# Graph layers 2 and 3 of a three-part network: second product in three rounded passes, and a new order of each graph's work

## The chip, the cores and the metric

The kernel runs on one core of one Trainium2 chip (trn2). TensorE is called PE below, VectorE DVE, ScalarE ACT, GpSimd POOL and SyncE SP. The metric is the device time of one execution in microseconds, as the median of the runs shown; lower is better.

## The reference

The program has four stages: masked attention, an LSTM, three graph layers, and a product with fp8 rounding. The change touches the graph stage and the load of one weight for the last. For 32 graphs of 256 nodes with 256 features each (D = 256), the graph stage computes

```python
for l in range(3):
    scores = (x @ attn_w[l, :d])[:, :, None] + (x @ attn_w[l, d:])[:, None, :] + attn_b[l]
    scores = jnp.where(scores >= 0, scores, 0.2 * scores)
    attn = jax.nn.softmax(jnp.where(mask, scores, -jnp.inf), axis=-1)
    agg = jnp.einsum('bij,bjd->bid', attn, x)
    h = layernorm(x + agg, g1[l], beta1[l])
    ff = gelu(h @ W1[l] + b1[l]) @ W2[l] + b2[l]      # W1: 256 x 1024, W2: 1024 x 256, all float32
    x = layernorm(h + ff, g2[l], beta2[l])
```

The stage's input is a layernorm of the residual stream, and its output is added to that stream. The last stage, which needs `L1_ffn_weight`, follows.

## The kernel before

`gnn_phase` holds the graph stage: 3 layers of 32 graphs, every tensor of a graph in SBUF. Each engine has its own program, and the order of the work is written out by hand in a function `body` per engine. One body is one graph's turn: `now` is the graph in the wide layer (`up`, gelu, `down`), `ahead` the next one, `soon` the one after, `behind` and `past` the two before. The engines are held together by semaphores alone, and each takes its own instructions in order.

What a graph n goes through: DVE's `as_neighbour` splits the per-node sums into two rounded parts; PE's `scores` (L1384, L1388) adds them to the mask in bank S; ACT's `attend` makes the slope part (Relu, L1086), DVE's `largest` (L1194, L1199) the row maximum, ACT the exponents (L1092); PE's `turn_probs` (L1400) transposes them into bank T, DVE's `turned` (L1211) copies them out; PE's `aggregate` (L1412) multiplies with the nodes; DVE's `aggregated` (L1221, L1227, L1231) adds the residual and takes mean and variance; POOL's `rsqrt1` (four tiny instructions, L975 to L980) makes the scale; ACT's `norm1` (L1116) applies it; PE's `turn_h` (L1421) transposes into bank T again; ACT's `hT_out` (L1138) and DVE's `split_hT` (L1238) turn that into two rounded halves, `hT_upper` and `hT_rest`. Only then may PE write bank T again or start `up`.

`up` (L1447) is W1 times h. Both operands are split into a rounded part of type float32r and the rest, also float32r, and three products are added up (upper x upper, upper x rest, rest x upper), 48 matmuls of 256 columns for a graph. ACT's `feed` (L1104) applies gelu bank by bank, four banks (q = 0 to 3) with two instructions of 256 columns each. `down` (L1464) is W2 times gelu in plain float32: 8 chunks times 2 halves are 16 matmuls, which PE executes as two each, 32 records for a graph. DVE's `feed` (L1265) adds h, `moments2` takes the statistics, POOL's `rsqrt2`, ACT's `norm2` (L1123), and POOL's `scale` and `move` (L1018, L1025) finish the layer.

ACT holds one function table at a time: exponents and gelu need different ones, so each turn has two table loads (at L1082 and L1104). In layer 1 the residual stream of a later graph also enters (POOL `enter`, L1031; `norm_extra`, L1129), and in layer 3 that of a finished graph leaves (POOL `leave`, L1036; L1129). At the edge of two layers `split_w1` (L1246, L1250) rounds the next W1, and PE's `shift_bias` (L1431) multiplies it with one column. `down` has this core, and the PE body this order:

```python
for it in range(NT):
    last = pe.matmul(ff_bank[:, it * D:(it + 1) * D], act1[:, m, it * P:(it + 1) * P], w2[:, m, :], ...)

scores(*ahead); up(*now, range(0, 6)); turn_probs(*ahead); up(*now, range(6, MC))
aggregate(*ahead); down(*now, range(0, 6)); turn_h(*ahead); down(*now, range(6, MC))
```

## Time and profile before

| | us |
|---|---|
| median of 3 runs (lowest to highest) | 3022.4 (3019.73 to 3022.41) |
| profiled execution, its time | 3024.76 |
| its span in the trace | 3023.0 |
| PE matmul busy | 2772.3 (92%) |
| ACT busy | 1784.0 (59%) |
| DVE busy | 1674.8 (55%) |
| POOL busy | 1503.2 (50%) |
| matmuls of `down`, 3072 records | 698.0 |
| matmuls of `up`, 3 x 1536 records | 442.6 + 435.0 + 434.7 |

The graph stage lies from about 1285 to 2906 us of the span. Matmuls are pipelined, so two of them overlap in these sums: the pace of PE is read from the start of one to the start of the next. The shares are averages over the four stages; the time of the graph stage is set by how long one body takes, times 96. TensorE's granted clock is at or near its full level in the graph stage.

### The profile page before, as it was taken

What the parts mean: (1) busy time and instruction counts of PE and PEld (TensorE: products, weight loads), DVE (VectorE), ACT (ScalarE), POOL (GpSimd) and SP (SyncE); (2) the same over time, 40 slices, a digit from 0 to 9 for tenths busy, and PEclk for the clock granted to TensorE, in tenths of its full rate; (3) what the DMA queues carried; (4) which work ended last, traced back from release to release, by engine and by line L of the source; (5) the groups of instructions that cost most, each with busy time, mean ns of one, the idle gap of its engine ahead of it and who ended that gap; (6) DMA issues with size and microseconds to landing.
All of it is one profiled execution on the core that took longest, in us unless ns stands there. A gap on an engine that the chain in (4) does not pass through costs nothing. (4 is left out here: it accounts for less than half of the span.)

```text
span 3023.0 us, 113835 instructions
## 1 busy us (share of the span) xinstructions
PE 2772.3 (92%) x43200; PEld 2452.8 (81%) x43200; DVE 1674.8 (55%) x5581; ACT 1784.0 (59%) x4834; POOL 1503.2 (50%) x2681
## 2 busy tenths in 40 slices
PE   6999999978888888769999999999999999999957
PEld 5777777667777777759889898999999899999956
DVE  6887888634444444446666664544444445454558
ACT  4666666644444444437667665666666577767723
POOL 5777777510000000046666665555555566666644
PEclk9999999999999999979999999999999999999979
DMA  2111111000000000020000011000000100000002
GB/s 88 43 35 35 35 43 35 13 11 12 13 13 12 13 13 13 13 73 26 26 21 26 24 30 48 9 9 7 9 9 7 34 9 9 9 7 9 9 21 90
DMA packets 110487, 72.32 MB, mean 24 GB/s; under 512 B 51424, under 2 KB 109280, under 8 KB 110432
## 3 DMA queue, kind: packets, MB, share of 16 engines
q1 hardware_dynamic: 96464, 58.93, 6.7%
q10 hardware_dynamic: 13968, 12.72, 1.4%
q8 instruction: 27, 0.44, 0.1%
q14 instruction: 28, 0.23, 0.0%
HBM read 50.63 MB, written 20.97 MB: 24 GB/s over the span
## 5 line engine op out<-in xcount | busy, mean ns | idle before, releaser
L1464 PE MATMUL g_F<-g_w,g_act 128*128 128x256 f32 x3072 | 698.0, 380 | 0.0
L1464 PEld LDWEIGHTS g_F<-g_w,g_act 128*128 128x128 f32 x3072 | 578.4, 191 | 75.1
L1447 PE MATMUL g_H<-g_hT_upper,g_w_upper 128*128 128x256 f32 x1536 | 442.6, 288 | 0.0
L1447 PE MATMUL g_H<-g_hT_upper,g_w_rest 128*128 128x256 f32 x1536 | 435.0, 283 | 0.0
L1447 PE MATMUL g_H<-g_hT_rest,g_w_upper 128*128 128x256 f32 x1536 | 434.7, 283 | 0.0
L744 POOL COPY l_xt<-seq 128x64 f32 x256 | 60.9, 238 | 597.5 <-PE l_O L755 595.8
L328 ACT ACTIVATE a_probs<-a_S,a_nmax 128x256 f32<-128x256 f32 x512 | 236.7, 480 | 123.2 <-DVE a_nmax L421 89.8
L1104 ACT ACTIVATE g_act<-g_H,g_small 128x256 f32<-128x256 f32 x768 | 291.4, 490 | 6.0 <-PE g_H L1447 4.8
L1447 PEld LDWEIGHTS g_H<-g_hT_upper,g_w_upper 128*128 128x128 f32 x1536 | 294.5, 192 | 0.1
L1447 PEld LDWEIGHTS g_H<-g_hT_upper,g_w_rest 128*128 128x128 f32 x1536 | 294.5, 192 | 0.0
L1447 PEld LDWEIGHTS g_H<-g_hT_rest,g_w_upper 128*128 128x128 f32 x1536 | 294.5, 192 | 0.0
L783 ACT ACTIVATE l_ic<-l_G 128x128 f32<-128x128 f32 x256 | 71.2, 278 | 342.2 <-PE l_G L755 342.2
L1116 ACT ACTIVATE g_r<-g_r,g_small 128x256 f32<-128x256 f32 x192 | 104.8, 593 | 274.3 <-POOL g_small L980 274.3
L755 PE MATMUL l_G<-wh,l_hT 128*32 128x128 f32 x4096 | 165.3, 279 | 106.5 <-DVE l_hT L817 106.0
L1001 POOL TENSOR_TENSOR g_h<-g_r,g_g_row 128x256 f32<-128x256 f32 x192 | 138.3, 742 | 233.3 <-DVE g_r L1265 233.3
L1238 DVE TENSOR_TENSOR g_hT_rest<-g_T,g_hT_upper 128x512 fp32r<-128x512 f32 x96 | 66.4, 692 | 338.8 <-ACT g_hT_upper L1138 338.8
L755 PEld LDWEIGHTS l_G<-wh,l_hT 128*32 128x32 f32 x4096 | 96.6, 109 | 147.6 <-DVE l_hT L817 147.5
L802 DVE SCALAR_TENSOR_TENSOR l_fresh<-l_ic 128x64 f32<-128x64 f32 x256 | 57.8, 226 | 278.3 <-ACT l_ic L783 278.3
L1018 POOL TENSOR_TENSOR g_r<-g_r,g_g_row 128x256 f32<-128x256 f32 x192 | 135.8, 729 | 146.2 <-ACT g_r L1123 146.2
L978 POOL TENSOR_TENSOR g_small<-g_small,eps_power 128x2 f32<-128x2 f32 x256 | 188.2, 735 | 20.0
L1412 PE MATMUL g_A<-seq,g_probsT 128*128 (+1 forms) x768 | 182.7, 381 | 0.8 <-DVE g_probsT L1211 0.8
L421 DVE TENSOR_REDUCE a_nmax<-a_S 128x2 f32<-128x512 f32 x256 | 157.3, 677 | 15.9 <-PE a_S L590 15.9
(207 smaller groups left out, 7244.3 us busy)
## 6 DMA issues: line engine op xcount, KB each, us to landing
gmask<-masks ACTq DMA_DIRECT2D x97, 128.0 KB, 2.0
x<-in_x_dram SPq DMA_DIRECT2D x32, 256.0 KB, 3.1
a_adj<-in_adj_dram SPq DMA_DIRECT2D x32, 256.0 KB, 2.7
hidden<-l_hs SPq DMA_DIRECT2D x512, 16.0 KB, 1.4
g_hs<-hidden SPq DMA_DIRECT2D x32, 256.0 KB, 2.7
out_dram<-q_res SPq DMA_DIRECT2D x32, 256.0 KB, 2.1
g_w<-in_L_gnn_W_dram SPq DMA_DIRECT2D x6, 1024.0 KB, 6.2
masks<-gmask SPq DMA_DIRECT2D x32, 128.0 KB, 1.7
```

Source lines behind the costliest of these rows:

```text
L328: last = act.activation(probs[h % PROBS][:, it, :], score_bank[h % HG][:, it * N:(it + 1) * N], ACT.Exp, bias=nmax[:, h, it:it + 1], accum ...
L421: dve.tensor_reduce(nmax[:, h, :], score_bank[h % HG][:, :].rearrange("p (t k) -> p t k", t=NT), AX.X, ALU.max, negate=True).then_inc(max_ ...
L755: last = pe.matmul(bank[j * B:(j + 1) * B, 0:(gates.stop - gates.start) * HQ], x[:, c, :], w[:, c, gates, j * HQ:(j + 1) * HQ], start=Fals ...
L783: act.activation(ic[:, :, :], ic_bank[u % 2][:, 0:2 * HQ], ACT.Tanh).then_inc(ic_done, 1)
L978: pool.tensor_tensor(rstd[:, :, 0], veps[:, :, 0], t.power[:, :], ALU.pow).then_inc(rstd_done, 1)
L1001: last = pool.tensor_tensor(h[:, it, :], r1[:, it, :], g1_row[:, :], ALU.mult)
L1018: last = pool.tensor_tensor(r2[:, it, :], r2[:, it, :], g2_row[:, :], ALU.mult)
L1104: last = act.activation(act1[:, 2 * q + i, :], hidden_bank[q][:, i * N:(i + 1) * N], ACT.Gelu, bias=b1_shifted[:, 2 * q + i:2 * q + i + 1])
L1116: last = act.activation(r1[:, it, :], r1[:, it, :], ACT.Identity, bias=nb1[:, it, :], scale=rstd1[:, it, :])
L1412: last = pe.matmul(agg_bank[:, it * D:(it + 1) * D], probsT[:, jt, it * P:(it + 1) * P], t.nodes[:, b, jt, :], start=(jt == 0), stop=(jt = ...
L1447: last = pe.matmul(hidden_bank[m // 2][:, m % 2 * N:(m % 2 + 1) * N], w[:, c, m * P:(m + 1) * P], x[:, c, :], start=(c == 0 and k == 0), s ...
L1464: last = pe.matmul(ff_bank[:, it * D:(it + 1) * D], act1[:, m, it * P:(it + 1) * P], w2[:, m, :], start=(m == 0 and it == 0), stop=(m == M ...
```

## The change

Four things change in `gnn_phase`, and one outside.

1. `down` in layers 2 and 3 takes the form of `up`: `w2_upper`, `w2_rest`, `act_upper` and `act_rest` are float32r, and each of the 16 matmuls becomes three, 48 for a graph. Layer 1 keeps plain float32. The rounded part of the gelus of a bank is made on ACT for the banks in `ON_ACT` (q = 1 and 3 in layer 2, q = 3 in layer 3) and on DVE for the others (`split_act`); the rest is always made on DVE. `split_w2` rounds W2 once a layer, and W2 is loaded in two halves.
2. The turns are reordered. `scores` and the slopes are made for `soon`, and the exponents of `soon` come last but one in ACT's turn, between `norm1(ahead)` and `hT_out(ahead)`; the gelus come first. PE begins a turn with `turn_probs(ahead)`, and `aggregate` stands in the middle of `up`. POOL puts `enter`/`leave` before `rsqrt2`, and `rsqrt1` before `scale`.
3. `scale` writes to `nodes`, so that `r2` is free after `scaled_done`, not after `nodes_done`.
4. W1 of layers 2 and 3 is loaded over the residual stream of four graphs, which is stored in HBM meanwhile; other buffers share memory too.
5. `L1_ffn_weight` is loaded at the start of the last stage, not at the end of the graph stage.

Core of the diff:

```diff
+        w2_rest, w2_upper = sb("w2_rest", [P, MC, D], F32R), sb("w2_upper", [P, MC, D], F32R)
...
+        act_rest, act_upper = sb("act_rest", [P, MC, N], F32R), sb("act_upper", [P, MC, N], F32R)
...
+        ON_ACT = ((), (1, 3), (3,))
...
+                    if l == 1:
+                        sp.wait_ge(extra_x, B)
+                        sp.dma_start(aside[:, :, :, :], lent).then_inc(aside_out, 16)
...
+                    sp.dma_start(w1_of(l), a["L1_gnn_W1"][l].rearrange("(c p) n -> p c n", p=P)).then_inc(w1_in, 16)
...
+                    after(sp, half_ps, l)
+                    sp.dma_start(w2_raw[:, 0:MC // 2, :], w2_src[:, 0:MC // 2, :]).then_inc(w2_half_in, 16)
                     after(sp, ff_ps, l * B)
-                    sp.dma_start(w2[:, :, :], a["L1_gnn_W2"][l].rearrange("(c p) n -> p c n", p=P)).then_inc(net_in, 16)
+                    sp.dma_start(w2_raw[:, MC // 2:MC, :], w2_src[:, MC // 2:MC, :]).then_inc(net_in, 16)
...
-                sp.dma_start(t.ffn_weight[:, :, :], a["L1_ffn_weight"].rearrange("(c p) n -> p c n", p=P)
-                             ).then_inc(t.ffn_weight_in, 16)
+                sp.wait_ge(w1_done, L)
+                sp.wait_ge(bias_done, L)
+                sp.dma_start(lent, aside[:, :, :, :]).then_inc(aside_in, 16)
...
-                def body(soon, ahead, now, behind, past):
+                def body(later, soon, ahead, now, behind, past):
                     e, gone = entering(now), leaving(past)
+                    residual(*now)
                     if e is not None:
                         enter(e)
                     if gone is not None:
                         leave(gone)
-                    residual(*now)
                     if behind:
                         rsqrt2(*behind)
                     residual_end(*now)
+                    if ahead:
+                        rsqrt1(*ahead)
+                    if behind:
+                        scale(*behind)
+                        move(*behind)
                     if e is not None:
                         rsqrt_extra(e)
                     if gone is not None:
                         rsqrt_extra(B + gone)
...
+                def slope(l, b):
+                    n = l * B + b
                     act.wait_ge(scores_ps, n + 1)
...
                     last.then_inc(slopes_done, 1)
+                def attend(l, b):
+                    n = l * B + b
+                    after(act, warm_done, n)
+                    act.activation(warm[:, :], t.eps[:, :], ACT.Exp).then_inc(warm_done, 1)
                     act.wait_ge(shift_done, n + 1)
                     after(act, turned_ps, n)
+                    after(act, rtotal_done, n)
...
                     last.then_inc(exp_done, 1)
-                def feed(l, b):
-                    n = l * B + b
-                    if isinstance(b, int) and b == 0:
-                        act.wait_ge(bias_done, l + 1)
-                    after(act, ff_ps, n)
-                    for q in range(NB):
+                def feed(l, b, part):
+                    n = l * B + b
+                    if part[0] == 0:
+                        if isinstance(b, int) and b == 0:
+                            act.wait_ge(bias_done, l + 1)
+                        after(act, ff_ps, n)
+                    for q in part:
                         act.wait_ge(hidden_ps, n * NB + q + 1)
                         for i in range(2):
...
+                        if q in ON_ACT[l]:
+                            act.wait_ge(gelu_done, n * NB + q + 1)
+                            act.activation(act_upper[:, 2 * q:2 * q + 2, :], act_raw[:, 2 * q:2 * q + 2, :],
+                                           ACT.Copy).then_inc(upper_by_act, 1)
...
-                def body(soon, ahead, now, behind, past):
-                    e, gone = entering(now), leaving(past)
-                    if ahead:
-                        attend(*ahead)
-                        load_mask(*ahead)
-                    feed(*now)
+                    slope(*soon)
+                    attend(*soon)
+                    load_mask(*soon)
+                def body(later, soon, ahead, now, behind, past):
+                    gone = leaving(past)
+                    if soon:
+                        slope(*soon)
+                        load_mask(*soon)
+                    feed(*now, range(0, 2))
                     if behind:
                         norm2(*behind)
-                    if e is not None:
-                        norm_extra(e, e)
-                    if gone is not None:
-                        norm_extra(B + gone, gone)
+                    if later and later[0] == 0:
+                        norm_extra(later[1], later[1])
+                    if gone is not None and not (isinstance(gone, int) and gone == 0):
+                        norm_extra(B + gone - 1, gone - 1)
+                    feed(*now, range(2, NB))
                     if ahead:
                         norm1(*ahead)
+                    if soon:
+                        attend(*soon)
+                    if ahead:
                         hT_out(*ahead)
...
+                def split_w2(l):
+                    for half, loaded in enumerate((w2_half_in, net_in)):
+                        dve.wait_ge(loaded, (l + 1) * 16)
+                        part = slice(half * MC // 2, (half + 1) * MC // 2)
+                        dve.tensor_copy(w2_upper[:, part, :], w2_raw[:, part, :]).then_inc(w2_upper_done, 1)
+                        dve.wait_ge(w2_upper_done, (l - 1) * 2 + half + 1)
+                        dve.tensor_tensor(w2_rest[:, part, :], w2_raw[:, part, :], w2_upper[:, part, :].bitcast(F32),
+                                          ALU.subtract).then_inc(w2_done, 1)
+                def split_act(l, b, part):
+                    n = l * B + b
+                    for q in part:
+                        span = slice(2 * q, 2 * q + 2)
+                        on_act = sum(k < q for k in ON_ACT[l])
+                        if q in ON_ACT[l]:
+                            dve.wait_ge(upper_by_act, before(l, act_uppers) + b * act_uppers(l) + on_act + 1)
+                        else:
+                            dve.wait_ge(gelu_done, n * NB + q + 1)
+                            dve.tensor_copy(act_upper[:, span, :], act_raw[:, span, :]).then_inc(upper_by_dve, 1)
+                            dve.wait_ge(upper_by_dve, before(l, dve_uppers) + b * dve_uppers(l) + q - on_act + 1)
+                        dve.tensor_tensor(act_rest[:, span, :], act_raw[:, span, :], act_upper[:, span, :].bitcast(F32),
+                                          ALU.subtract).then_inc(act_done, 1)
...
-                    after(dve, nodes_done, n)
+                    after(dve, scaled_done, n)
...
-                def body(soon, ahead, now, behind, past):
+                def body(later, soon, ahead, now, behind, past):
                     e, gone = entering(now), leaving(past)
+                    crossing = ahead and now[0] < ahead[0]
+                    if ahead:
+                        turned(*ahead)
                     if behind:
                         feed(*behind)
-                    if ahead:
-                        largest(*ahead)
+                    if soon:
+                        largest(*soon)
                     if behind:
+                        stats2_of(*behind)
                         moments2(*behind)
-                    if past and gone is None:
-                        next_pair(*past)
                     if ahead:
                         reciprocals(*ahead)
-                        turned(*ahead)
+                    if in_parts(now[0]):
+                        if isinstance(now[1], int) and now[1] == 0:
+                            split_w2(now[0])
+                        split_act(*now, range(0, 1))
+                    if ahead:
+                        aggregated(*ahead)
+                    if in_parts(now[0]):
+                        split_act(*now, range(1, NB))
+                    if later and later[0] == 0:
+                        pair_entered(later[1])
+                    if later:
+                        as_neighbour(*later)
+                    if crossing:
+                        split_w1(ahead[0])
                     if e is not None:
                         moments_extra(e, e)
                     if gone is not None:
+                        if not (isinstance(gone, int) and gone == 0):
+                            most_left(B + gone - 1, gone - 1)
                         moments_extra(B + gone, gone)
-                    if soon:
-                        as_neighbour(*soon)
-                    if ahead:
-                        aggregated(*ahead)
-                    if ahead and now[0] < ahead[0]:
-                        split_w1(ahead[0])
-                    if e is not None:
-                        pair_entered(e)
-                    if gone is not None:
-                        most_left(B + gone, gone)
+                    if past and gone is None and not crossing:
+                        next_pair(*past)
...
+                        first = isinstance(b, int) and b == 0 and m % (MC // 2) == 0
+                        if in_parts(l):
+                            if m % 2 == 0:
+                                pe.wait_ge(act_done, before(l, banks) + b * NB + m // 2 + 1)
+                            if first:
+                                pe.wait_ge(w2_done, (l - 1) * 2 + m // (MC // 2) + 1)
+                            products = ((act_upper, w2_upper), (act_rest, w2_upper), (act_upper, w2_rest))
+                        else:
+                            if m % 2 == 0:
+                                pe.wait_ge(gelu_done, n * NB + m // 2 + 1)
+                            if first:
+                                pe.wait_ge((w2_half_in, net_in)[m // (MC // 2)], 16)
+                            products = ((act_raw, w2_raw),)
                         for it in range(NT):
+                            for k, (x, w) in enumerate(products):
+                                last = pe.matmul(ff_bank[:, it * D:(it + 1) * D], x[:, m, it * P:(it + 1) * P], w[:, m, :],
+                                                 start=(m == 0 and it == 0 and k == 0),
+                                                 stop=(m == MC - 1 and k == len(products) - 1), skip_group_check=True)
+                        if isinstance(b, int) and b == B - 1 and l < L - 1 and m == MC // 2 - 1:
+                            last.then_inc(half_ps, 1)
...
-                def body(soon, ahead, now, behind, past):
-                    if ahead:
-                        scores(*ahead)
-                    up(*now, range(0, 6))
+                def body(later, soon, ahead, now, behind, past):
                     if ahead:
                         turn_probs(*ahead)
-                    up(*now, range(6, MC))
+                    if soon:
+                        scores(*soon)
+                    up(*now, range(0, 4))
                     if ahead:
                         aggregate(*ahead)
+                    up(*now, range(4, MC))
                     down(*now, range(0, 6))
                     if ahead:
                         turn_h(*ahead)
+                    down(*now, range(6, MC))
                     if ahead and now[0] < ahead[0]:
                         shift_bias(ahead[0])
-                    down(*now, range(6, MC))
...
-        weight = t.ffn_weight
+        weight = sb("weight", [P, KC, D])
...
+                sp.dma_start(weight[:, :, :], a["L1_ffn_weight"].rearrange("(c p) n -> p c n", p=P)).then_inc(t.ffn_weight_in, 16)
```

ACT, the loop of layer 2, one turn. Before (g_act is the gelus, g_H the banks of `up`, g_r the buffers r1 and r2):

```order
L1082 ACT_TABLE_LOAD
L1082 ACTIVATE g_small<-eps_power 128x2 [waits g_warm_done]
...
L1086 ACTIVATE g_slopes<-g_S,g_small 128x256 [waits g_scores_ps]
...
L1092 ACTIVATE g_probs,g_small<-g_slopes,g_small 128x256 [waits g_turned_ps,g_shift_done]
...
L1104 ACT_TABLE_LOAD
L1104 ACTIVATE g_act<-g_H,g_small 128x256 [waits g_hidden_ps]
...
L1123 ACTIVATE g_r<-g_r,g_small 128x256 [waits g_nb2_done]
...
L1116 ACTIVATE g_r<-g_r,g_small 128x256 [waits g_nb1_done]
...
L1138 ACTIVATE g_hT_upper<-g_T 128x512 [waits g_hidden_ps]
```

Now, from the last bank of gelus to the end of the turn:

```order
L1159 ACTIVATE g_act_raw<-g_H,g_small 128x256 [waits g_hidden_ps]
L1159 ACTIVATE g_act_raw<-g_H,g_small 128x256
L1166 ACTIVATE g_act_upper<-g_act_raw 128x512 [waits g_gelu_done]
L1175 REGISTER_ALU
L1177 ACTIVATE g_r<-g_r,g_small 128x256 [waits g_nb1_done]
L1177 ACTIVATE g_r<-g_r,g_small 128x256
L1141 ACT_TABLE_LOAD
L1141 ACTIVATE g_small<-eps_power 128x2 [waits g_warm_done]
L1146 ACTIVATE g_probs,g_small<-g_slopes,g_small 128x256 [waits g_rtotal_done,g_turned_ps,g_shift_done]
L1146 ACTIVATE g_probs,g_small<-g_slopes,g_small 128x256
L41 ISA [waits g_hT_ps]
L1199 ACTIVATE g_hT_upper<-g_T 128x512 [waits g_hidden_ps]
```

The table load and the exponents stood ahead of the gelus and now stand between `norm1` and `hT_out`, and a copy of 512 columns has come in behind the gelus of bank 3.

DVE, the loop of layer 2, from the sum after `aggregate` on. Before:

```order
L1221 SCALAR_TENSOR_TENSOR g_r<-g_A,g_small,seq 128x256
L1227 BN_STATS g_small<-g_r 128x6 [waits g_r1_done]
L1227 BN_STATS g_small<-g_r 128x6
L1231 BN_AGGR g_small<-g_small 128x2 [waits g_stats1_done]
L1231 BN_AGGR g_small<-g_small 128x2
L1238 TENSOR_TENSOR g_hT_rest<-g_T,g_hT_upper 128x512 [waits g_hT_upper_done]
```

Now:

```order
L1301 BN_AGGR g_small<-g_small 128x2 [waits g_stats1_done]
L1301 BN_AGGR g_small<-g_small 128x2
L1346 TENSOR_TENSOR g_act_rest<-g_act_raw,g_act_upper 128x512 [waits g_upper_by_act]
L1343 REGISTER_ALU
L1344 CAST g_act_upper<-g_act_raw 128x512 [waits g_gelu_done]
L1345 REGISTER_ALU
L1346 TENSOR_TENSOR g_act_rest<-g_act_raw,g_act_upper 128x512 [waits g_upper_by_dve]
L1346 TENSOR_TENSOR g_act_rest<-g_act_raw,g_act_upper 128x512 [waits g_upper_by_act]
L1252 REGISTER_ALU
L1254 ISA [waits g_slopes_done,g_pair_done]
```

Where DVE had nothing between the aggregation and `split_hT`, four instructions on SBUF operands now follow the aggregation directly, at the place where POOL runs `rsqrt1`.

## Rows read from the trace of the kernel before

**Rows 1.** PE in layer 2, one turn. Start us, duration us, engine, line, operation, count.

```profile
2211.65 0.38 PE L1384 MATMUL g_S<-gmask,identb 128*128 128x512 bf16 x1
...
2212.33 0.28 PE L1447 MATMUL g_H<-g_hT_upper,g_w_upper 128*128 128x256 f32 x1
...
2216.65 0.60 PE L1400 MATMUL g_T<-ident,g_probs 128*128 128x128 f32 x4
...
2218.51 1.89 PE L1412 MATMUL g_A<-seq,g_probsT 128*128 x8
2220.24 5.34 PE L1464 MATMUL g_F<-g_w,g_act 128*128 128x256 f32 x24
2225.48 0.66 PE L1421 MATMUL g_T<-ident,g_r 128*128 128x128 f32 x4
...
2227.70 0.38 PE L1384 MATMUL g_S<-gmask,identb 128*128 128x512 bf16 x1
```

**Rows 2.** ACT in the same turn, timeline.

```profile
2214.58 0.51 ACT L1092 ACTIVATE g_probs<-g_slopes,g_small 128x256 f32<-128x256 f32 x1 [1.21 <-DVE g_small L1199]
...
2215.69 1.28 ACT L1104 ACT_TABLE_LOAD   x1
2216.99 3.03 ACT L1104 ACTIVATE g_act<-g_H,g_small 128x256 f32<-128x256 f32 x8
...
2224.34 1.09 ACT L1116 ACTIVATE g_r<-g_r,g_small 128x256 f32<-128x256 f32 x2 [3.34 <-POOL g_small L980]
2226.25 0.60 ACT L1138 ACTIVATE g_hT_upper<-g_T 128x512 fp32r<-128x512 f32 x1 [0.83 <-PE g_T L1421]
...
2228.16 0.20 ACT L1082 ACTIVATE g_small<-eps_power 128x2 f32<-128x2 f32 x1
```

**Rows 3.** DVE in the same turn, timeline.

```profile
2222.52 0.31 DVE L1231 BATCH_NORM_AGGREGATE g_small<-g_small 128x2 f32<-128x6 f32 x2
2226.88 0.69 DVE L1238 TENSOR_TENSOR g_hT_rest<-g_T,g_hT_upper 128x512 fp32r<-128x512 f32 x1 [4.05 <-ACT g_hT_upper L1138]
```

**Rows 4.** POOL in the same turn, timeline.

```profile
2212.71 1.44 POOL L1001 TENSOR_TENSOR g_h<-g_r,g_g_row 128x256 f32<-128x256 f32 x2 [3.10 <-DVE g_r L1265]
...
2222.91 0.20 POOL L975 TENSOR_TENSOR g_small<-g_small,eps_power 128x2 f32<-128x2 f32 x1 [0.42 <-DVE g_small L1231]
...
2224.11 0.20 POOL L980 TENSOR_TENSOR g_small<-g_small 128x2 f32<-128x2 f32 x1
```

**Rows 5.** DVE at the edge of layers 1 and 2, timeline.

```profile
1845.63 2.48 DVE L1250 SCALAR_TENSOR_TENSOR g_w_rest<-g_w,g_small,g_w_upper 128x1024 fp32r<-128x1024 f32 x2
```

**Rows 6.** POOL at the same edge, timeline.

```profile
1845.72 1.75 POOL L978 TENSOR_TENSOR g_small<-g_small,eps_power 128x2 f32<-128x2 f32 x1
1847.55 0.61 POOL L980 TENSOR_TENSOR g_small<-g_small 128x2 f32<-128x2 f32 x1
```

**Rows 7.** POOL in layer 1, two turns, timeline.

```profile
1602.92 1.27 POOL L1031 TENSOR_TENSOR x<-x,g_hs 128x512 f32 x1
...
1619.29 1.27 POOL L1031 TENSOR_TENSOR x<-x,g_hs 128x512 f32 x1
```

**Rows 8.** ACT in layer 3, timeline.

```profile
2615.18 1.12 ACT L1129 ACTIVATE seq<-x,g_small  x2
```

**Rows 9.** POOL in layer 3, two turns, timeline.

```profile
2604.17 1.27 POOL L1036 TENSOR_TENSOR x<-x,seq  x1 [0.21 <-POOL seq L1025]
...
2620.11 1.27 POOL L1036 TENSOR_TENSOR x<-x,seq  x1 [0.21 <-POOL seq L1025]
```

**Rows 10.** DVE in the first stage, a rounding of 512 columns, timeline.

```profile
14.22 0.39 DVE L502 CAST a_wq_upper<-a_probsT 128x512 fp32r<-128x512 f32 x1
```

**Rows 11.** PE at the edge of layers 1 and 2, timeline.

```profile
1849.84 5.31 PE L1431 MATMUL g_A<-g_small,g_w 128*128 128x1 f32 x32
```

**Rows 12.** DVE at the start of the last stage, timeline.

```profile
2906.64 0.68 DVE L1632 TENSOR_REDUCE q_most<-ffn_weight 128x1 f32<-128x512 f32 x1
```

**Rows 13.** Page, part 6: DMA issues with KB each and us to landing.

```profile
g_hs<-hidden SPq DMA_DIRECT2D x32, 256.0 KB, 2.7
```

126 lines of the change are left out of this document (77 added, 49 removed).

## The prediction

> **What bounds the kernel now.** I read the page first for where the time lies, then one steady turn of layer 2 on each engine in turn, because the graph stage is 96 such turns. On PE [rows 1] a turn runs from one `scores` to the next, 2211.65 to 2227.70, 16.05 us, and no row waits: 0.68 for `scores`; 4.32 for the first 36 matmuls of `up`, 0.12 each; 1.86 for `turn_probs` and the other 12, so `turn_probs` takes 0.42; 1.73 for `aggregate`; 5.24 for 24 records of `down`, 0.218 each; 2.22 for `turn_h` and the last 8, so `turn_h` takes 0.47. The others wait for PE or for each other: `norm1` on ACT stood idle 3.34 before it, `split_hT` on DVE 4.05 [rows 2, 3]. So PE alone sets layer 2. In layer 1 a turn takes 16.37 [rows 7] and in layer 3 15.94 [rows 9].
>
> **What PE saves.** `down` in float32 is 32 records of 0.218, 6.98; three rounded passes are 48 matmuls of the shape that `up` has, 5.76. PE's work in a turn of layers 2 and 3 falls from 16.05 to 14.82. If PE stayed the bound this would be 1.23 x 60 steady turns, 74 us. The question is what is late next.
>
> **The new loop of waits.** I put t = 0 at the start of `turn_probs`, which now begins PE's turn and may not start before `split_hT` of the turn before has freed bank T. PE then runs 0.42 + 0.68, 24 matmuls of `up` (2.88), `aggregate` from 3.98 (1.73), 24 more (2.88), and ends `up` at 8.59. A last matmul ends about 0.16 after its slot (2218.51 + 1.89 against 2220.24) and ACT follows 0.11 later (2225.48 + 0.66, then 2226.25) [rows 1, 2], so ACT can begin the gelus of bank 3 at 8.86. A pair of gelus takes about 0.85 (eight take 3.03 [rows 2]), to 9.7. Then, in ACT's order, the copy of bank 3, priced at 0.60 by `hT_out`, the nearest copy of that shape [rows 2], and a wait of ACT for its own gelu (no row; 0 to 0.2, I take 0.1). So `norm1` can start at S = 10.4. From S to the next `turn_probs` everything stands in one line: `norm1` 1.09, table load 1.28, the warming exponent 0.20, the exponents 1.11 (2214.58 to 2215.69), `hT_out` 0.60 [rows 2], `split_hT` 0.69 [rows 3], and some 0.2 for five hand-overs, 5.15 in all. The turn is S + 5.15, at least 15.55, and no longer PE's 14.82. PE's own part after `up` (48 matmuls and `turn_h`, 6.23) is hidden under this. That the exponents stand behind `norm1` and ahead of `hT_out` costs 2.6 of the chain; before they stood ahead of the gelus. The change thus cannot give more than 0.5 in a turn of layer 2 and 0.4 in one of layer 3, unless ACT's part is shorter than its rows.
>
> **What S waits for in layer 2.** `norm1` also needs `rsqrt1` from POOL. DVE's aggregation ended 4.32 after `aggregate` began (2218.51 to 2222.83 [rows 1, 3]), so now at 8.30; `rsqrt1` took 1.40 undisturbed (2222.91 to 2224.31 [rows 4]), so 9.8, earlier than 10.4. But DVE now does four things on SBUF operands from 8.3 on: the rest of bank 1 (0.69, as `split_hT`), the rounding of bank 2 (0.39 [rows 10]), its rest (0.69), and at 10.5, behind ACT's copy, the rest of bank 3. At the edge of two layers the trace shows what such a DVE instruction does to `rsqrt1`: of two that took 2.48 together [rows 5], the first ended at about 1846.87, and POOL's power, which had been issued at 1845.72, ended 0.6 after that, at 1847.47; its last small multiply, 0.20 when alone [rows 4], took 0.61 and ended 0.05 after the second [rows 6]. So each small POOL instruction gets in only where a DVE instruction ends. Laid over the new order: first one at 9.05, second at 9.5, the power can read at 10.2 and ends at 10.8, and the last meets the rest of bank 3 (10.5 to 11.2). S is 11.15, the turn 16.3. The ends are S = 10.4 (POOL slips in everywhere) and 11.7 (the power too waits for the bank 3 instruction): 15.55 to 16.85. I take 16.3, since in the rows no small POOL instruction slipped in.
>
> The Trainium skill, "SBUF — State Buffer", section "Who interferes with whom", says that a VectorE instruction with two SBUF inputs, or in a two-port mode, and a GpSimd instruction exclude each other for the whole instruction; the edge rows agree with it. The same section says that a VectorE instruction with at most one SBUF input outside those modes does not contend; if the new instructions behaved so, the turn would be the one of the first rival.
>
> **What S waits for in layer 3.** DVE rounds bank 1 as well, and POOL's `leave` (1.27 [rows 9]) now stands ahead of `rsqrt2`. DVE's sum r2 ends at about 2.0, `residual` takes 1.44 [rows 4], to 3.55, `leave` to 4.85, `rsqrt2` alone to 6.3. ACT's `norm2` and `norm_extra` (1.12 for one [rows 8], some 2.0 together) end at 8.3, before bank 3 is ready; S = 10.5, the turn 15.65. But DVE's rounding and rest of bank 0 (0.39 + 0.69) fall on `rsqrt2`, which then ends at 7.0; ACT comes to bank 2 at 9.0, to the end of bank 3 at 10.6, and S is 11.15 again, the turn 16.3 against 15.94.
>
> **Layer 1** has no rounding of gelus and PE's old sum of 16.05. Chain: S is about 10.2, and `hT_out` must wait for `turn_h`, which ends at 14.3; the next `turn_probs` could start at 16.0. So PE is the bound, and 16.37 becomes 16.05. `rsqrt1` no longer waits behind the moments of the entering graph.
>
> **The rest.** The first body comes later, by one more small group on POOL (1.4) and one more set of moments on DVE ahead of the first `norm1`: 1.4 to 3.5, I take 2.4. The weight of the last stage is first read at 2906.64 [rows 12], with nothing waited for; issued at the stage's start, it lands 2.7 later, as a load of its size does [rows 13]: +2.5. The two edges of layers keep the 5.31 of `shift_bias` [rows 11], which now covers a `split_hT` (-1.5), and gain `split_w2` ahead of bank 0 (two roundings and two rests of 1024 columns, 4.3 by twice the 0.39 and 0.69 of [rows 3, 10]); the old edge lost some 2.4 where `rsqrt1` was held up [rows 5, 6]. I take 0, bounds -6 and +8. The SP loads around them (two halves of W2, the four graphs set aside) land in the time of whole turns or under `shift_bias`. The last turn is shorter by its `down`, -1.2. The earlier release of r2 saves nothing, since DVE's r2 waits for PE.
>
> **Sum.** Layer 1: -0.32 x 30 = -9.6. Layer 2: +0.25 x 30 = +7.5. Layer 3: +0.36 x 30 = +10.8. The rest: +3.7. In all +12.4 on the profiled execution's own 3024.8, which is 3037.2; that execution is 2.4 above the median of the runs, so the median should be **3035**.
>
> **Rivals.**
> 1. POOL is not held up. For it: the gaps between DVE's instructions are real, the roundings are short. Against it: the edge rows. Layer 2 at 15.55 (-15.0) and layer 3 at 15.65 (-8.7): 3024.8 - 9.6 - 15.0 - 8.7 + 3.7 = 2995, as a median 2993. This is the faster side; it decides where the power reads before the rest of bank 2 starts, at t = 9.6. Chance 0.19.
> 2. Only one layer is held up. Layer 2 free and layer 3 as forecast gives 3012, the other way round 3015. Chance 0.24.
> 3. PE stays the bound, because ACT's line overlaps more than its rows show. It would need 0.75 less: 60 x 1.23 and 9.6 less, 3.7 more, 2943. Chance 0.03.
> 4. Held up more: the power waits for bank 3's instruction too, turns of 16.8 in both layers, some 30 us more than forecast, 3050 to 3065. Chance 0.07.
> 5. The pieces cancel, turns at about 16.1: 3018 to 3028. Chance 0.07.
>
> **How the numbers follow.** The forecast itself, turns of 16.2 to 16.5, has 0.40, and gives 3029 to 3046. A measurement of this kernel can tell about 0.2%, 6 us, from no change. Faster by more: rival 1, rival 3 and 0.14 of rival 2, 0.36. Within: 0.10 of rival 2, rival 5 and 0.03 of the forecast, 0.20. Slower by more: 0.44. The range 2992 to 3050 leaves out rival 3, half of rival 1 and half of rival 4.
>
> **What would show it.** Right: in layers 2 and 3 PE waits once a turn, at `turn_probs`, for `split_hT`, by 0.7 to 1.6 us; ACT waits at `norm1` for POOL; `rsqrt1` takes well over 1.40; `down` runs at 0.12 a matmul; layer 1 turns at 16.05. Wrong: PE without a wait, a table load or copy on ACT that costs no time of its own, or PE waiting inside `down` for a rest (by my table the rests of banks 0 to 3 come 0.4 us or more before PE wants them). If the granted clock fell where PE now waits, the turns would be longer than every case here.

## The result, and the profile of the changed kernel

The changed kernel takes 2994.6 us, median of four runs (2992.4 to 2997.8), against 3022.4: a ratio of 0.991, with a 95% interval of 0.9894 to 0.9925. The forecast was 3035, slower by 12; it is faster by 28. The time lies inside the range, near its lower end. It is almost the time of the first rival (2993), but not its mechanism: POOL was held up in layer 2 and did not matter in layer 3, which is the second case of the second rival (3015). The rest of the way to 2995 is made up of smaller errors: 8 us in layer 2, 7 at the edges, 3 in layer 1, 2 at the start.

The profiled execution took 2992.5 (span 2990.7), 32.3 less than that of before. The starts of `aggregate`, one for each graph, cut the two traces into the same pieces:

| piece | before | changed | difference | forecast |
|---|---|---|---|---|
| attention and LSTM stages, to the first `aggregate` | 1309.30 | 1304.53 | -4.8 | 0 |
| start of the graph stage, to the second | 24.72 | 25.14 | +0.4 | +2.4 |
| layer 1, 31 turns | 506.15 | 493.98 | -12.2 | -9.6 |
| edge of layers 1 and 2, 3 turns | 57.06 | 55.31 | -1.8 | 0 |
| layer 2, 29 turns | 465.54 | 464.66 | -0.9 | +7.5 |
| edge of layers 2 and 3, 3 turns | 58.63 | 53.86 | -4.8 | (in the 0 above) |
| layer 3, 28 turns | 446.69 | 436.86 | -9.8 | +10.8 |
| from the last `aggregate` to the end | 154.91 | 156.36 | +1.4 | +2.5, -1.2 |

The first row is scatter and not the change: ACT's first instruction of the LSTM's steps already began at 615.29 and not 620.45, behind a stage that the change doesn't touch, and over the kernels of this document the first `aggregate` began anywhere between 1304.5 and 1311.4. So 27.5 of the 32.3 belong to the graph stage and what follows, which agrees with the 27.8 between the medians.

A steady turn takes 15.93 in layer 1 (16.37 before), 16.01 in layer 2 (16.05) and 15.66 in layer 3 (15.95). By the page PE has lost 89 us of work (2683.2 busy) and DVE has gained 378 (2052.4), and the time went down by 32. Busy times by stretch in layers 1, 2 and 3 (columns: stretch, its length, busy us and count of PE, PEld, DVE, ACT, POOL, granted clock, DMA share, GB/s):

```profile
1400.00:1800.00 400.00, 400.00 (x2509) 368.64 (x2533) 289.04 (x1049) 285.37 (x601) 281.12 (x523) 1.00 0.09 28
1900.00:2300.00 400.00, 372.50 (x2899) 361.28 (x2924) 329.54 (x900) 291.53 (x600) 252.88 (x400) 1.00 0.03 8
2400.00:2800.00 400.00, 381.25 (x2971) 369.81 (x2994) 324.69 (x869) 302.07 (x641) 319.90 (x538) 1.00 0.03 8
```

PE is busy all of the time in layer 1, and idle for 27.5 of 400 in layer 2 and 18.8 in layer 3. One turn of layer 2, timeline, starts in us: PE, ACT, DVE and POOL. They answer to [rows 1 to 4].

```profile
2099.09 0.66 PE L1513 MATMUL g_T<-ident,g_probs 128*128 128x128 f32 x4 [1.10 <-DVE g_hT_rest L1308]
...
2115.10 0.66 PE L1513 MATMUL g_T<-ident,g_probs 128*128 128x128 f32 x4 [1.09 <-DVE g_hT_rest L1308]
```

```profile
2108.80 0.63 ACT L1166 ACTIVATE g_act_upper<-g_act_raw 128x512 fp32r<-128x512 f32 x1
2110.25 1.09 ACT L1177 ACTIVATE g_r<-g_r,g_small 128x256 f32<-128x256 f32 x2 [0.81 <-POOL g_small L1029]
2111.36 1.28 ACT L1141 ACT_TABLE_LOAD   x1
2112.65 0.20 ACT L1141 ACTIVATE g_small<-eps_power 128x2 f32<-128x2 f32 x1
2112.76 0.50 ACT L1146 ACTIVATE g_probs<-g_slopes,g_small 128x256 f32<-128x256 f32 x1
...
2113.75 0.57 ACT L1199 ACTIVATE g_hT_upper<-g_T 128x512 fp32r<-128x512 f32 x1
```

```profile
2107.30 0.66 DVE L1346 TENSOR_TENSOR g_act_rest<-g_act_raw,g_act_upper 128x512 fp32r<-128x512 f32 x1
...
2108.33 0.69 DVE L1346 TENSOR_TENSOR g_act_rest<-g_act_raw,g_act_upper 128x512 fp32r<-128x512 f32 x1
2109.47 0.69 DVE L1346 TENSOR_TENSOR g_act_rest<-g_act_raw,g_act_upper 128x512 fp32r<-128x512 f32 x1 [0.45 <-ACT g_act_upper L1166]
...
2114.35 0.69 DVE L1308 TENSOR_TENSOR g_hT_rest<-g_T,g_hT_upper 128x512 fp32r<-128x512 f32 x1 [0.31 <-ACT g_hT_upper L1199]
```

```profile
2107.46 0.55 POOL L1024 TENSOR_TENSOR g_small<-g_small,eps_power 128x2 f32<-128x2 f32 x1 [0.37 <-DVE g_small L1301]
2107.97 0.38 POOL L1025 TENSOR_TENSOR g_small<-g_small,eps_power 128x2 f32<-128x2 f32 x1
2108.42 1.16 POOL L1027 TENSOR_TENSOR g_small<-g_small,eps_power 128x2 f32<-128x2 f32 x1
2109.66 0.56 POOL L1029 TENSOR_TENSOR g_small<-g_small 128x2 f32<-128x2 f32 x1
```

PE waits 1.09 at `turn_probs` for `split_hT`, and no other row of the turn has a wait. From `norm1` (2110.25) to that point ACT and DVE work in one line, and `norm1` itself waited 0.81 for `rsqrt1`, whose four small instructions took 2.76 (2107.46 to 2110.22) where they took 1.40 before [rows 4]. The first, the second and the last end within 0.06 of the end of a DVE instruction on SBUF operands: the last, started at 2109.66, at 2110.22, beside the rest of bank 3 (2109.47 to 2110.16). The power (0.70 when alone) ends 0.56 after the rest of bank 2 (2108.33 to 2109.02).

Layer 3, one turn, ACT, POOL and the end of the turn on PE:

```profile
2603.33 1.09 ACT L1184 ACTIVATE g_r<-g_r,g_small 128x256 f32<-128x256 f32 x2 [1.63 <-POOL g_small L1029]
...
2605.31 1.54 ACT L1159 ACTIVATE g_act_raw<-g_H,g_small 128x256 f32<-128x256 f32 x4
...
2607.42 1.08 ACT L1177 ACTIVATE g_r<-g_r,g_small 128x256 f32<-128x256 f32 x2
```

```profile
2604.96 0.29 POOL L1024 TENSOR_TENSOR g_small<-g_small,eps_power 128x2 f32<-128x2 f32 x1 [0.28 <-DVE g_small L1301]
...
2606.70 0.66 POOL L1029 TENSOR_TENSOR g_small<-g_small 128x2 f32<-128x2 f32 x1
```

```profile
2612.27 0.66 PE L1513 MATMUL g_T<-ident,g_probs 128*128 128x128 f32 x4 [0.75 <-DVE g_hT_rest L1308]
```

Here `norm1` follows the copy without a wait: ACT came to bank 2 at 2605.31, after `norm2` and `norm_extra`, and `rsqrt1`, although held up too (2.40), ended just before `norm1` began (2607.36, 2607.42).

### The profile page after: what moved, and what is told of

The parts are those of the page before. It is cut to its first block and busy times, and to the rows that moved or that the text cites. A ratio compares the mean times of both kernels' runs of the same rounds, so it can differ in the third digit from the quotient of the medians.

```text
span 2990.7 us, 116485 instructions
## 1 busy us (share of the span) xinstructions
PE 2683.2 (90%) x44066; PEld 2435.4 (81%) x44224; DVE 2052.4 (69%) x6005; ACT 1839.8 (62%) x4930; POOL 1620.6 (54%) x2681
## 5 line engine op out<-in xcount | busy, mean ns | idle before, releaser
L1560 PE MATMUL g_H<-g_hT_upper,g_w_upper 128*128 128x256 f32 x1536 | 453.9, 295 | 0.0
L1159 ACT ACTIVATE g_act_raw<-g_H,g_small 128x256 f32<-128x256 f32 x768 | 303.3, 469 | 22.2 <-PE g_H L1560 21.0
L1587 PE MATMUL g_F<-g_w_upper,g_act_upper 128*128 128x256 f32 x1024 | 293.1, 286 | 4.5 <-DVE g_act_rest L1346 4.1
L1587 PE MATMUL g_F<-g_w_upper,g_act_rest 128*128 128x256 f32 x1024 | 288.0, 281 | 0.0
L1587 PE MATMUL g_F<-g_w_rest,g_act_upper 128*128 128x256 f32 x1024 | 287.5, 281 | 0.0
L1027 POOL TENSOR_TENSOR g_small<-g_small,eps_power 128x2 f32<-128x2 f32 x256 | 234.0, 914 | 20.0
L1587 PE MATMUL g_F<-g_w_raw,g_act_raw 128*128 128x256 f32 x1024 | 231.5, 379 | 0.0
L1133 ACT ACTIVATE g_slopes<-g_S,g_small 128x256 f32<-128x256 f32 x192 | 80.7, 472 | 213.2 <-PE g_S L1501 213.2
L1346 DVE TENSOR_TENSOR g_act_rest<-g_act_raw,g_act_upper 128x512 fp32r<-128x512 f32 x256 | 191.1, 748 | 25.8 <-ACT g_act_upper L1166 20.0
L1587 PEld LDWEIGHTS g_F<-g_w_raw,g_act_raw 128*128 128x128 f32 x1024 | 189.6, 190 | 23.2
```

The lines of the kernel that those rows point to most:

```text
L1027: pool.tensor_tensor(rstd[:, :, 0], veps[:, :, 0], t.power[:, :], ALU.pow).then_inc(rstd_done, 1)
L1133: last = act.activation(slopes[:, it, :], score_bank[:, it * N:(it + 1) * N], ACT.Relu, bias=knee[:, it:it + 1], scale=-0.8)
L1159: last = act.activation(act_raw[:, 2 * q + i, :], hidden_bank[q][:, i * N:(i + 1) * N], ACT.Gelu, bias=b1_shifted[:, 2 * q + i:2 * q + i + 1])
L1346: dve.tensor_tensor(act_rest[:, span, :], act_raw[:, span, :], act_upper[:, span, :].bitcast(F32), ALU.subtract).then_inc(act_done, 1)
L1560: last = pe.matmul(hidden_bank[m // 2][:, m % 2 * N:(m % 2 + 1) * N], w[:, c, m * P:(m + 1) * P], x[:, c, :], start=(c == 0 and k == 0), s ...
L1587: last = pe.matmul(ff_bank[:, it * D:(it + 1) * D], x[:, m, it * P:(it + 1) * P], w[:, m, :], start=(m == 0 and it == 0 and k == 0), stop= ...
```

## The experiments

Starts of `aggregate` give each kernel's turns without the scatter of the first stages. In us, each layer's steady turn; the graph stage is from the second `aggregate` to the last, 94 turns:

| kernel | layer 1 | layer 2 | layer 3 | graph stage | median of runs |
|---|---|---|---|---|---|
| before | 16.37 | 16.05 | 15.95 | 1534.1 | 3022.4 |
| changed | 15.93 | 16.01 | 15.66 | 1504.7 | 2994.6 |
| e1 order alone, float32 | 15.94 | 15.94 | 15.93 | 1505.7 | 2997.3 |
| e2 bank 1 of layer 2 on DVE | 15.93 | 15.56 | 15.65 | 1490.5 | 2984.4 |
| e3 without rests of banks 1 to 3 | 15.93 | 15.10 | 15.66 | 1475.8 | 2966.4 |
| e4 hT_out ahead of exponents | 16.60 | 15.03 | 14.75 | 1468.4 | 2959.3 |
| e5 rests held back | 15.93 | 16.04 | 16.70 | 1547.7 | 3040.5 |
| e6 exponents first | 17.25 | 17.47 | 17.04 | 1623.6 | 3117.9 |
| e7 combined | 15.94 | 14.98 | 14.70 | 1446.4 | 2938.4 |
| e8 combined, float32 | 15.94 | 15.94 | 15.94 | 1507.7 | 2997.0 |
| e9 bank 1 of layer 3 on ACT | 15.93 | 16.02 | 15.67 | 1506.1 | 2995.8 |

### e1: the order without the three passes

```diff
-        ON_ACT = ((), (1, 3), (3,))
+        ON_ACT = ((), (), ())
         def in_parts(l):
-            return l > 0
+            return False
```

(and the waits on W2 count its loads of all three layers).

> The changed kernel with its new order of work on every engine, but with the second product in plain float32 in all three layers (32 matmuls, no rounding, no rests, no splitting of W2). Theory (the order carries the gain and PE is the bound without the three passes): PE's own work is 15.93 a turn, as in layer 1 of the changed kernel, and the chain over ACT is shorter than that, so all three layers turn at 15.93: layer 2 0.08 below the changed kernel (16.01), layer 3 0.27 above it (15.66), the two edges some 2 shorter each without the split of W2. About 2996. Rival (the three passes carry the gain, the order nothing): layers 2 and 3 as in the kernel before, 16.05 and 15.95, with its edges; about 3008 or more.

Measured 2997.3, ratio 0.9916 (0.9899 to 0.9932). The stretches of layers 2 and 3 as above:

```profile
1900.00:2300.00 400.00, 400.00 (x2536) 368.78 (x2536) 211.48 (x762) 266.33 (x553) 217.14 (x404) 1.00 0.03 8
2400.00:2800.00 400.00, 400.00 (x2535) 368.73 (x2534) 199.69 (x675) 285.69 (x604) 263.58 (x528) 1.00 0.03 8
```

PE never idles, and every layer turns at its 15.94. So 25 of the 28 us (by the medians) come from the rest of the change, above all the order of work (by pieces of the profiled executions 12 in layer 1, 12 at the two edges, 5 in layers 2 and 3). No run measures the parts of the new order, or items 3 to 5 of the change, one by one against before. For layer 1 the trace of before tells what went: its last turns, in which no graph enters, already ran at 15.95 and not 16.37, and in the others PE waited for `norm1`:

```profile
1619.15 0.66 PE L1421 MATMUL g_T<-ident,g_r 128*128 128x128 f32 x4 [0.22 <-ACT g_r L1116]
```

In the changed kernel no row of PE in a steady turn of layer 1 has a wait. The three passes, which take 1.2 off PE in each of 64 turns, bring 1 us of the graph stage (1505.7 against 1504.7; 3 by the medians): 0.27 a turn gained in layer 3, 0.08 lost in layer 2, and at each edge 2.5 lost to `split_w2` (three turns 52.81 here against 55.31, and 51.32 against 53.86).

### e2: the place of one rounding

```diff
-        ON_ACT = ((), (1, 3), (3,))
+        ON_ACT = ((), (3,), (3,))
```

> The changed kernel with one number different: in layer 2 the rounding of bank 1 stands on DVE, as in layer 3, and no longer on ACT. Theory (the order of DVE's instructions against rsqrt1 sets layer 2): the rounding lies beside POOL's first two small instructions and lets them in, as in layer 3 (0.29 and 0.19 in place of 0.55 and 0.38), rsqrt1 ends 0.35 earlier, and layer 2 turns at 15.65 to 15.70 in place of 16.01; 30 turns of 0.33, about 2985. Rival (DVE's amount of work sets it): DVE gets 0.42 more in a turn, and layer 2 turns at 16.0 to 16.4; 2995 to 3006.

Measured 2984.4, ratio 0.987 (0.9854 to 0.9887), as the theory had it; layer 2 turned at 15.56, a little better than 15.65. POOL in one turn of layer 2:

```profile
2200.51 0.29 POOL L1024 TENSOR_TENSOR g_small<-g_small,eps_power 128x2 f32<-128x2 f32 x1 [0.38 <-DVE g_small L1301]
...
2201.02 1.02 POOL L1027 TENSOR_TENSOR g_small<-g_small,eps_power 128x2 f32<-128x2 f32 x1
2202.12 0.48 POOL L1029 TENSOR_TENSOR g_small<-g_small 128x2 f32<-128x2 f32 x1
```

DVE does 0.42 more in a turn and the turn is 0.45 shorter. `rsqrt1` takes 2.09 in place of 2.76, since what follows the aggregation directly is now a rounding of 0.40 (2200.35 to 2200.75) in place of a rest of 0.66, and the first small instruction ends just behind it.

### e3: without the rests

```diff
-                        dve.tensor_tensor(act_rest[:, span, :], act_raw[:, span, :], act_upper[:, span, :].bitcast(F32),
-                                          ALU.subtract).then_inc(act_done, 1)
+                        if q == 0:
+                            dve.tensor_tensor(...).then_inc(act_done, 1)
+                        else:
+                            dve.sem_inc(act_done, 1)
...
-                            products = ((act_upper, w2_upper), (act_rest, w2_upper), (act_upper, w2_rest))
+                            products = ((act_upper, w2_upper), (act_rest if m < 2 else act_upper, w2_upper), (act_upper, w2_rest))
```

This kernel leaves out part of the work: the correction by the rests of banks 1 to 3 is missing from its product, and PE runs as many matmuls as in the changed kernel, with the rounded half in place of the rest.

> The changed kernel without DVE's rests of banks 1 to 3 in layers 2 and 3 (the subtraction of 512 columns is left out, the pass that would read it reads the rounded half instead, so PE does the same number of matmuls). Theory (the rests on SBUF operands hold rsqrt1 up): rsqrt1 falls from 2.76 to between 1.4 and 1.9, norm1 then waits for ACT's own line and starts at 10.3 to 10.5 after turn_probs in layer 2, turn 15.2 to 15.4; in layer 3 ACT's line was already level with POOL, turn 15.5 to 15.65. About 2970 to 2978. Rival (POOL is slow there for another reason): rsqrt1 stays at 2.4 to 2.8 and the time at 2990 to 2995.

Measured 2966.4, ratio 0.9814 (0.9798 to 0.983), 4 below the lower end of what was expected. Timeline of POOL and ACT in layer 2:

```profile
2203.30 0.20 POOL L1024 TENSOR_TENSOR g_small<-g_small,eps_power 128x2 f32<-128x2 f32 x1 [0.36 <-DVE g_small L1301]
...
2204.75 0.20 POOL L1029 TENSOR_TENSOR g_small<-g_small 128x2 f32<-128x2 f32 x1
```

```profile
2205.18 1.08 ACT L1177 ACTIVATE g_r<-g_r,g_small 128x256 f32<-128x256 f32 x2
```

`rsqrt1` takes 1.65, `norm1` follows the copy of bank 3 at 10.25 after `turn_probs`, and the turn is 15.10: exactly what is left when POOL isn't held up, and 4.85 behind `norm1` as in the changed kernel. DVE also does 2.1 less in a turn here; e5, with all of the work, shows `norm1` at the same place. In layer 3 nothing changes (15.66), so there POOL was not what counted.

### e4: the exponents behind hT_out

```diff
                     if soon:
-                        attend(*soon)
+                        warm_up(*soon)
                     if ahead:
                         hT_out(*ahead)
+                    if soon:
+                        attend(*soon, alone_too=False)
...
-                    if ahead:
-                        turn_probs(*ahead)
                     if soon:
                         scores(*soon)
-                    up(*now, range(0, 4))
+                    up(*now, range(0, 2))
+                    if ahead:
+                        turn_probs(*ahead)
+                    up(*now, range(2, 4))
```

(DVE's `turned` goes behind `feed` and `largest`, and `slope` also waits for the exponents before.)

> The changed kernel with hT_out ahead of the exponents on ACT (the warming exponent and so the table load stay where they are), turn_probs behind the first 12 matmuls of up on PE, and turned behind feed and largest on DVE. Theory (the exponents in the chain between norm1 and the next turn_probs set the turn): the chain loses some 1.1 and layers 2 and 3 turn at PE's own 14.82 to 14.95; 30 turns of 1.1 and 30 of 0.75 less, about 2940. Rival 1 (DVE or POOL is the next bound close by, DVE is busy for some 13.3 of a turn): 15.3 to 15.6, 2970 to 2985. Rival 2 (the exponents are covered by something else): 2990 to 2995.

Measured 2959.3, ratio 0.9791 (0.9775 to 0.9807). Layers 2 and 3 did nearly as the theory said (14.82 to 14.95), 15.03 and 14.75; the 19 us that are missing were lost where none were expected, in layer 1, whose turn went from 15.93 to 16.60. DVE, POOL and PE there:

```profile
1512.15 1.02 DVE L1275 TENSOR_SCALAR g_small<-g_small 128x2 f32<-128x2 f32 x1
1513.09 0.68 DVE L1287 COPY g_probsT<-g_T 128x512 f32<-128x512 f32 x1
```

```profile
1511.86 1.29 POOL L1081 TENSOR_TENSOR x<-x,g_hs 128x512 f32 x1
```

```profile
1513.90 1.99 PE L1531 MATMUL g_A<-seq,g_probsT 128*128 x8 [0.40 <-DVE g_probsT L1287]
```

DVE's `shift` works on two columns and takes 0.17 when alone. Beside POOL's `enter` (1511.86 to 1513.15) it took 1.02 and ended with it; `turned`, now behind it in the queue, came late, and PE waited 0.40 at `aggregate`. This is the exclusion of [rows 5, 6] the other way round.

### e5: the same work, the rests held back

```diff
-                        split_act(*now, range(0, 1))
+                        split_act(*now, range(0, 2))
...
-                        split_act(*now, range(1, NB))
+                        split_act(*now, range(2, NB), ahead)   # the rest of bank 2 waits for nb1_done
```

> The changed kernel with all of its work, DVE's splits in another order in layers 2 and 3: rounding and rest of bank 1 stand ahead of the aggregation, and the rest of bank 2 waits until rsqrt1 is done (the bank 3 rest stands behind it). Nothing on SBUF operands but the rounding of bank 2 then lies beside rsqrt1. Theory (SBUF instructions of DVE hold rsqrt1 up): rsqrt1 takes 1.4 to 1.9 in place of 2.76, in layer 2 norm1 starts at 10.3 to 10.6 after turn_probs although its input comes 0.5 later, and layer 2 turns at 15.15 to 15.5; in layer 3 norm1 waits for ACT's own line, 15.65 as now, or up to 15.8 where the aggregation comes 0.9 later. 2970 to 2985. Rival (the mere amount of DVE work, or its lateness, sets the turn): the later aggregation shows in full, layer 2 at 16.3 to 16.5, 3005.

Measured 3040.5, ratio 1.0061 (1.0044 to 1.0077): a miss. Layer 2, POOL, ACT and DVE:

```profile
2207.87 0.32 POOL L1024 TENSOR_TENSOR g_small<-g_small,eps_power 128x2 f32<-128x2 f32 x1 [0.67 <-DVE g_small L1301]
...
2209.18 0.20 POOL L1029 TENSOR_TENSOR g_small<-g_small 128x2 f32<-128x2 f32 x1
2209.41 1.88 POOL L1068 TENSOR_TENSOR seq<-g_r,g_g_row 128x256 f32 x2
```

```profile
2209.47 1.08 ACT L1177 ACTIVATE g_r<-g_r,g_small 128x256 f32<-128x256 f32 x2
...
2213.00 0.60 ACT L1199 ACTIVATE g_hT_upper<-g_T 128x512 fp32r<-128x512 f32 x1
```

```profile
2209.49 2.35 DVE L1348 TENSOR_TENSOR g_act_rest<-g_act_raw,g_act_upper 128x512 fp32r<-128x512 f32 x2 [1.36 <-POOL g_small L1029]
...
2214.52 0.68 DVE L1308 TENSOR_TENSOR g_hT_rest<-g_T,g_hT_upper 128x512 fp32r<-128x512 f32 x1
```

The first half of the theory held to 0.1: `rsqrt1` took 1.51 (2207.87 to 2209.38) and `norm1` started at 10.25 after `turn_probs` (2199.22) instead of 11.16. But the two rests that were held back met POOL's `scale` instead and took 2.35 for 1.29 (the length of such a pair in e6, at 2206.55), the two small instructions behind them 0.70 and 0.79 for 0.16 and 0.22, and DVE reached `split_hT` at 2214.52, 0.9 after `hT_out` had ended. The chain was shortened and DVE's own queue took its place: 16.04, and 16.70 in layer 3. In the changed kernel that queue is 0.31 ahead of `hT_out`, which is all the room there is.

### e6: the exponents in their old place

```diff
                         slope(*soon)
                         load_mask(*soon)
+                        attend(*soon)
                     feed(*now, range(0, 2))
...
-                    if soon:
-                        attend(*soon)
                     if ahead:
                         hT_out(*ahead)
```

(and DVE's `reciprocals` at the head of its turn.)

> The changed kernel with the exponents where they stood before the change, ahead of the gelus (and DVE's reciprocals at the head of its turn), all else as changed. What the chain loses behind norm1 (2.6 for table load, warming and exponents) comes in front of the gelus (2.4), so that the rests of banks 0 and 1 come 0.8 late for down and the aggregation and rsqrt1 move back by 1.5. Theory: layers 2 and 3 turn at 15.6 to 15.9, PE waits inside down and not at turn_probs; 2985 to 2995. Rival (the exponents' new place was the cost that ate the gain of the three passes): PE's 14.8 to 15.1, 2945 to 2955. Rival on the other side (late gelus block down for good): 16.5 or more, 3015.

Measured 3117.9, ratio 1.0316 (1.0299 to 1.0334), beyond all three; the last rival has the turns (16.5 or more), but not the time. PE in a turn of layer 2, then DVE (`hT_out` ended at 2210.67):

```profile
2206.24 0.38 PE L1585 MATMUL g_F<-g_w_upper,g_act_upper 128*128 128x256 f32 x1 [0.97 <-DVE g_act_rest L1345]
```

```profile
2209.93 1.00 DVE L1380 SCALAR_TENSOR_TENSOR g_product<-seq,g_aw 128x256 f32<-128x256 f32 x1
...
2211.73 0.68 DVE L1307 TENSOR_TENSOR g_hT_rest<-g_T,g_hT_upper 128x512 fp32r<-128x512 f32 x1
```

PE waits twice. The 0.97 inside `down`, for the rest of bank 1, is about what was expected (0.8). The second is the queue of DVE again: the products of `next_pair`, 0.42 each when alone, take 0.72 to 1.00 beside POOL's `scale` and `move`, and `split_hT` starts at 2211.73, 1.06 after `hT_out` had ended. My sum had priced DVE's work at its undisturbed durations.

Nor does this need the three passes. Layer 1, which has none, goes from 15.93 to 17.25 as well, some 34 of the 119 us between the graph stages, in the turns in which a graph enters (its last three take 15.93). DVE and PE there (`hT_out` had ended at 1602.58):

```profile
1603.94 0.68 DVE L1307 TENSOR_TENSOR g_hT_rest<-g_T,g_hT_upper 128x512 fp32r<-128x512 f32 x1
```

```profile
1604.68 0.66 PE L1511 MATMUL g_T<-ident,g_probs 128*128 128x128 f32 x4 [1.09 <-DVE g_hT_rest L1307]
```

So with the new order around them the exponents' old place is worse by 1.3 to 1.5 a turn in every layer, with the passes or without. That doesn't clear the new place: e4 shows that the exponents do cost the chain 0.9 to 1.0 a turn in layers 2 and 3. It shows that going back to the old place is no cure.

### e7 and e8: a shorter chain, with and without the three passes

e7 is e4 with the `ON_ACT` of e2 and with `shift` behind `moments2`:

```diff
-                    dve.wait_ge(top_done, n + 1)
-                    dve.tensor_scalar(shift[:, :], top[:, :], -1.0, None, ALU.mult).then_inc(shift_done, 1)
+                def shift_out(l, b):
+                    dve.wait_ge(top_done, l * B + b + 1)
+                    dve.tensor_scalar(shift[:, :], top[:, :], -1.0, None, ALU.mult).then_inc(shift_done, 1)
...
                         moments2(*behind)
+                    if soon:
+                        shift_out(*soon)
```

> The kernel with hT_out ahead of the exponents, with bank 1 of layer 2 rounded on DVE, and with DVE's small shift behind moments2 and no longer between largest and turned. In the kernel with hT_out ahead alone, layer 1 went from 15.93 to 16.60 a turn because that small shift took 1.02 beside POOL's enter (0.17 alone) and held turned up, and PE's aggregate with it. Theory: layer 1 comes back to 15.93 (30 turns of 0.67, 18 less), layer 2 from 15.03 to 14.75 to 14.9, layer 3 stays at 14.7 to 14.8; about 2934. Rival (another instruction of layer 1 keeps turned late): layer 1 at 16.3 to 16.6, 2950 to 2955.

Measured 2938.4, ratio 0.9722 (0.9706 to 0.9739). Layers 2 and 3:

```profile
1900.00:2300.00 400.00, 399.66 (x3133) 387.33 (x3133) 351.60 (x989) 300.41 (x616) 272.00 (x429) 1.00 0.03 9
2400.00:2700.00 300.00, 300.00 (x2392) 294.40 (x2391) 249.03 (x692) 245.39 (x512) 256.75 (x430) 1.00 0.03 9
```

Layer 1 is back at 15.94, so the `shift` beside `enter` was the whole of e4's loss, and PE has next to no gap left in any layer (400.00 of 400 in layer 1). Layer 2 stays 0.08 above what was expected and 0.27 above layer 3. Busy times don't show that, since the records of matmuls overlap: in the turn looked at, the first matmul of `up` starts at 2103.88, just behind `split_hT` (2103.07 to 2103.75), which DVE's products kept waiting. This kernel is 56 us faster than the changed one.

e8 is e7 with the second product in float32, by the edit of e1.

> The combined kernel (hT_out ahead of the exponents, the shift behind moments2) with the second product in plain float32 in all layers, so the shortened chain without the three passes. Theory (with float32 PE is the bound at 15.93 whatever the chain, and the three passes pay only where the chain is shorter than PE's work): all three layers turn at 15.93 and the time is that of the changed order in float32, 2993 to 3000, so that the three passes are worth 3 in the changed kernel and near 59 here. Rival (the shortened chain gains by itself): below 2985.

Measured 2997.0, ratio 0.9919 (0.9902 to 0.9935). With float32 the shortened chain brings nothing (e1 had 2997.3); with the shortened chain the three passes bring 59. In the changed kernel they brought 3.

### e9: layer 3 with the rounding of layer 2

```diff
-        ON_ACT = ((), (1, 3), (3,))
+        ON_ACT = ((), (1, 3), (1, 3))
```

> The changed kernel with one number different: layer 3 rounds bank 1 on ACT, as layer 2 does, and no longer on DVE. DVE then does less, and ACT's copy falls into its wait for rsqrt2. Theory (what stands directly behind the aggregation on DVE decides whether POOL's small instructions get in; a rest shuts them out, a rounding lets them in): rsqrt1 in layer 3 goes from 2.40 to about 2.76 and layer 3 turns at 15.95 to 16.05, as layer 2 does; about +10, 3004. Rival (layer 3 is set by ACT's own line, which loses nothing here, or by the amount of DVE work, which falls): layer 3 at 15.5 to 15.7, 2990 to 2996.

Measured 2995.8, ratio 0.9917 (0.99 to 0.9933): the theory fell and the rival held. ACT and POOL in layer 3:

```profile
2607.77 1.54 ACT L1159 ACTIVATE g_act_raw<-g_H,g_small 128x256 f32<-128x256 f32 x4
...
2609.88 1.08 ACT L1177 ACTIVATE g_r<-g_r,g_small 128x256 f32<-128x256 f32 x2
```

```profile
2607.41 0.55 POOL L1024 TENSOR_TENSOR g_small<-g_small,eps_power 128x2 f32<-128x2 f32 x1 [0.28 <-DVE g_small L1301]
```

The first small instruction is shut out here as in layer 2 (0.55), but `rsqrt1` ends after 2.41 (at 2609.82), as without the edit. Bank 2's gelus come later than in layer 2, behind `norm_extra`, DVE idles 0.70 before it can round that bank, and POOL gets through in that gap. `norm1` follows ACT's copy at 10.82 after `turn_probs`. POOL and ACT arrive together here too (2609.82, 2609.88); that it is ACT's own line which sets layer 3 is shown by e3, where POOL was freed and the turn stayed.

## Why the prediction went wrong, step by step

**PE's part: right.** PE's work was to fall to 14.82; layer 3 of e7 turns at 14.70, layer 2 at 14.98. In layers 2 and 3 PE waits once a turn, at `turn_probs`, for `split_hT`, by 1.09 and 0.75. Bank 3's gelus were to start at 8.86 after `turn_probs` and started at 8.84 (2107.93).

**S in layer 2: right.** S is the time from `turn_probs` to `norm1`. 11.15 was the forecast, 11.16 is measured, by the mechanism named: the power ended 0.56 after the bank 2 rest (0.6), the last multiply met the rest of bank 3. The rest of bank 2 and the power came 0.3 earlier than in my table (the power ended at 10.49 and not 10.8), which cost nothing, as the last multiply still waited for bank 3. e3 and e5 show it from both sides, both with 10.25 once nothing stands in POOL's way (forecast 10.4).

**The line behind S: mis-sized, and that was the sign of layer 2.** This is the largest step that failed. I had 5.15 (its terms add up to 5.17) from `norm1` to the next `turn_probs`; it is 4.85 in the changed kernel and in e3. From start to start the rows give 1.11, 1.29, 0.11, 0.99, 0.60 and 0.75. Three terms fail by 0.1 each: the warming exponent (0.20 taken, and the next instruction starts after 0.11), the pair of exponents (1.11 taken, to the end of the last accumulator read, and `hT_out` starts after 0.99), and the hand-overs (0.2 taken, 0.09 found). I added durations, where ACT starts an instruction before the one ahead has ended. The turn was to be 16.3, 0.25 above before, and is 16.01, 0.04 below: 8.4 us. With it falls the bound of 0.5 on what a turn of layer 2 could gain, and the 15.55 of rival 1: with POOL out of the way e3 turns at 15.10, 0.95 below before.

**Layer 3: the wrong bound.** The step that failed is the one that carried layer 2's S over to layer 3. ACT was to come to bank 2 at 9.0 and to the end of bank 3 at 10.6, behind an `rsqrt2` that ended at 7.0, and S was put at 11.15 again (10.6 with the copy and the wait of the layer 2 sum would have been 11.3). ACT came to bank 2 at 8.71 and to the end of bank 3 at 10.25, since `rsqrt2` ended at 6.69, and the copy took it to S = 10.82 with no wait for POOL. The undisturbed case of the same paragraph, S = 10.5 and 15.65 a turn, had the turn to 0.01 with two errors that cancel: S is 10.82, and the line behind it 4.85. And the later bank 2 moves DVE's rests off POOL, which I had not seen (e9). 0.64 a turn is 18 of the 45 us between forecast and result; about half of it (0.30) is the line behind S again, and 0.34 the wrong S.

**Layer 1: right in kind, 2.6 more in size.** PE is the bound; its sum with the float32 product is 15.93 (layer 1 of the changed kernel, all layers of e1). The 16.05 had come from layer 2 of before, where I had read no wait; the longer part is `turn_h`, which began at 2225.48, as `norm1` ended (2225.43), a wait that the overlap of the records hides.

**The edges: the clock was left out.** I kept 5.31 for `shift_bias`. In the trace of before, PE had waited 2.11 for `norm1` shortly ahead of it, and the granted clock fell to the lower of its two levels (1.2 GHz) while it ran (0.92 on average from 1849 to 1852, then 0.50); now it runs at the upper one (2.4 GHz), and takes 3.63, in e1 too. The eight records of `down` behind it took 3.60 in before, where eight take 1.89 at the upper level. That the wait of 2.11 brought the clock down is not shown: in the changed kernel the clock falls as well, only later (last section). PE's wait before, then stretches inside the two, columns as above, first of before and then of the changed kernel, with PE's record there:

```profile
1849.35 0.66 PE L1421 MATMUL g_T<-ident,g_r 128*128 128x128 f32 x4 [2.11 <-ACT g_r L1116]
```

```profile
1852.00:1855.00 3.00, 3.00 (x15) 3.00 (x16) 0.00 (x0) 0.15 (x1) 0.00 (x0) 0.50 0.00 0
```

```profile
1835.00:1838.00 3.00, 3.00 (x27) 2.92 (x25) 0.38 (x1) 0.00 (x0) 0.41 (x1) 1.00 0.35 109
```

```profile
1835.59 3.63 PE L1544 MATMUL g_A<-g_small,x 128*128 128x1 f32 x32
```

The passes with `split_w2` cost 2.5 an edge by e1, where I had 4.3 before what it overlaps. In all the two edges gained 6.5.

**Start and end.** The start cost 0.4 and not 2.4. At the end the last graphs took 2.9 more up to the last r2, not less. PE waits 0.35 and 1.36 in the last two `down` for rests, but the splits are not the cause of the 2.9: in e1, which has none, it is the same 24.8 from the last `aggregate` to the last r2 (21.9 before). So it comes with the new order; which part of it is open. From the last r2 to the first reduction of the last stage it then took 1.7 less. The wait for the last stage's weight is in the trace (2.30), but the stage's next step, `q_floor`, came only 0.4 later behind the first reduction than before (6.17 against 5.78), because it waits for POOL as well.

**The whole.** That the three passes could hardly pay in this order was forecast (at most 0.5 and 0.4 a turn, itself too low a bound for layer 2), and e1 and e8 show it. That the rest of the change would bring 25 us was not: I had it at about 6 (9.6 less in layer 1, 3.7 more for the start, edges and end). The terms miss by 8.4 (layer 2), 20.6 (layer 3), 2.6 (layer 1), 6.5 (edges), 2.0 (start), -0.2 (end) and 4.8 (scatter), together the 45 between 12.4 and -32.3; nearly all on the same side. By steps, the line behind S is 17 of it (0.30 in 57 turns) and the S of layer 3 is 10. That the time still lay inside the range is in part luck: its low end stood for rival 1, POOL not held up, which is not what happened in layer 2.

## What to carry to other kernels

A product that is made cheaper on the bound engine gives only what the next chain leaves: here 1.2 a turn of PE became 3 us in all, and 59 once the chain had been shortened; so look for the second bound before paying for the first. Sum a chain by distances from start to start, each from rows of the same neighbours, and a queue's work by durations as they are beside the other engine, since a stall that is moved away from one instruction lands on another. And run the new order without the new arithmetic once: it says which of the two carries the gain.

## What the runs showed of the hardware

The exclusion of DVE and POOL on SBUF operands works both ways and spares no size: a two-column DVE instruction of 0.17 took 1.02 beside a POOL addition of 1.29, products of 0.42 took up to 1.00, and POOL's power of 0.70 and last multiply of 0.20 took 1.64 and 1.20 beside the splits of W2 (changed kernel, 1844.95 and 1846.67). The Trainium skill, "SBUF — State Buffer", section "Who interferes with whom", says that a VectorE instruction with two SBUF inputs contends with a GpSimd instruction that reads SBUF, and that one in a two-port mode shuts it out for the whole instruction; the durations above agree for the rests and products. No row names the mode in which the two-column `shift` and the rounding run, but both were held up (1.02 for 0.17; in e6 a rounding took 0.88 for 0.40 beside POOL's addition at 2201.08) or held POOL up.

The granted clock also fell where PE's rows show no wait. In the changed kernel it was 0.89 of full speed from 1838 to 1841, behind the 32 one-column matmuls of `shift_bias`, 0.54 in the next 3 us, and full again after that, with PE busy for 3.00 of each 3. While it was down the matmuls of `up` started 0.21 apart and not 0.12:

```profile
1841.00:1844.00 3.00, 3.00 (x16) 3.00 (x16) 2.82 (x13) 1.29 (x2) 1.42 (x2) 0.54 0.14 44
```
